# Weights requested in the first turn, and the first image's attention on four pairs of PSUM banks

## The reference

```
Q = Wq x + bq;  K = Wk x + bk;  V = Wv x + bv
attn = softmax(Q^T K / sqrt(128))          # 1024 x 1024 for each image
x = attn V + x
```

## Time and profile before

| | |
|---|---|
| device time, median of 3 runs | 8342.78 us (8341.23 to 8348.9) |
| span of the profiled execution | 8342.4 us |
| TensorE busy | 7778.2 us, 93% |
| GpSimd busy | 7494.7 us, 90% |
| VectorE busy | 7384.7 us, 89% |
| ScalarE busy | 7209.6 us, 86% |
| start of TensorE's first instruction | 22.78 us |
| start of the second turn (image 0) | 134.8 us |

### The profile page before, as it was taken

One profiled execution on the slowest core, in us unless ns is written; L12 is line 12 of the kernel. 1 busy time (PEld: TensorE's weight loads), 2 busy tenths in 40 slices (PEclk: granted clock), 3 DMA queues, 4 the chain that ended last, 5 costly groups with the idle time before them and its releaser, 6 DMA issues. The chain is left out here.

```text
span 8342.4 us, 152469 instructions
## 1 busy us (share of the span) xinstructions
PE 7778.2 (93%) x53376; PEld 6086.4 (73%) x53376; DVE 7384.7 (89%) x10476; ACT 7209.6 (86%) x12224; POOL 7494.7 (90%) x7020
## 2 busy tenths in 40 slices
PE   6999999999999999999999999999999999999986
PEld 4777777777777777777777777777777777777765
DVE  4899999999899999999988999999899999889885
ACT  5898898898888898888888888988889888889874
POOL 3999999999999999999899999999899999899985
PEclk9999999999999999999999999999999999999998
DMA  1222222222222222222222222222222222222221
GB/s 51 75 65 81 76 75 75 72 72 77 75 74 75 72 72 78 75 74 75 68 76 75 75 75 72 73 77 75 73 75 72 73 76 76 73 71 71 77 71 35
DMA packets 322661, 604.29 MB, mean 72 GB/s; under 512 B 42017, under 2 KB 45026, under 8 KB 321890
## 3 DMA queue, kind: packets, MB, share of 16 engines
q1 hardware_dynamic: 321890, 594.45, 23.0%
HBM read 556.55 MB, written 20.97 MB: 69 GB/s over the span
## 5 line engine op out<-in xcount | busy, mean ns | idle before, releaser
L1096 POOL TENSOR_TENSOR g<-h,c_all 128x1024 f32<-128x1024 f32 x2048 | 4858.1, 2372 | 455.0 <-PE ps L530 250.7
L864 ACT ACTIVATE da<-dt,a_neg 128x512 f32<-128x512 f32 x4096 | 2792.6, 714 | 201.2 <-DVE h L1197 195.6
L1197 DVE TENSOR_TENSOR_SCAN h<-da,ps 128x512 f32<-128x512 f32 x2048 | 2423.9, 1208 | 377.6 <-PE ps L526 219.1
L1197 DVE TENSOR_TENSOR_SCAN h<-da,h,ps 128x512 f32<-128x512 f32 x2048 | 2552.0, 1269 | 127.6 <-PE ps L526 48.6
L526 PE MATMUL ps<-ident,ub 128*128 128x128 f32 x16384 | 2397.3, 276 | 240.4 <-DVE h L1197 221.8
L526 PEld LDWEIGHTS ps<-ident,ub 128*128 128x128 f32 x16384 | 1878.9, 142 | 890.3 <-issue 495.6
L530 PE MATMUL ps<-ident,g 128*128 128x128 f32 x16384 | 2253.8, 275 | 14.5 <-POOL g L1096 11.0
L530 PEld LDWEIGHTS ps<-ident,g 128*128 128x128 f32 x16384 | 1897.9, 142 | 462.6 <-issue 431.4
L1082 POOL TENSOR_SCALAR ub<-u_tok,b_tok 128x256 f32<-128x256 f32 x4096 | 1929.3, 486 | 183.1 <-ACT u_tok L953 99.5
L876 ACT ACTIVATE ub<-u_tok,b_tok 128x256 f32<-128x256 f32 x4096 | 1839.6, 498 | 136.9 <-PE ps L526 121.3
L853 ACT ACT_TABLE_LOAD x446 | 572.2, 1283 | 7.9
(11 more groups left out here) (130 smaller groups left out, 9368.8 us busy)
## 6 DMA issues: line engine op xcount, KB each, us to landing
c_all<-c_rows SPq DMA_DIRECT2D x2048, 256.0 KB, 3.1
x_in<-in_x SPq DMA_DIRECT2D x32, 512.0 KB, 5.6
t_old<-t SPq DMA_DIRECT2D x32, 512.0 KB, 4.4
out<-tile_b SPq DMA_DIRECT2D x32, 512.0 KB, 2.9
c_rows<-rows SPq DMA_DIRECT2D x128, 32.0 KB, 2.9
w_conv<-in_conv_rows SPq DMA_DIRECT2D x1, 512.0 KB
f_w<-in_f_w SPq DMA_DIRECT2D x2, 256.0 KB
hid<-in_in_proj SPq DMA_DIRECT2D x1, 256.0 KB
```

The source lines that it names most:

```text
L864: act.activation(da[:, n % 2, half, :], dt[:, slot, half, :], ACT.Exp, scale=a_neg[:, r, half, s:s + 1]).then_inc(da_made, 1)
L1096: pool.tensor_tensor(g[:, n % 2, :, :], h[:, n % 2, :, at:at + BANK], c_all[:, n % RING, :].unsqueeze(1).to_broadcast([P, NH, BANK]), ALU.mult
L1197: dve.tensor_tensor_scan(h[:, n % 2, half, at:at + BANK], da[:, n % 2, half, :], ps[:, DB + half, :], before, ALU.mult, ALU.add).then_inc( ...
```

## The change

Three edits. The list `loads` is built ahead of the first block, and SP issues it in the first turn (before its first wait there) and no longer in the first block. In the first turn `att(i)` goes round four pairs of banks (X, Y and the two that the mixer uses in later turns, DB and YA), and scores wait for the addition of block i-4. The slots of the first turn put the scores of block i+2 between the transposes and the product of block i, and the set-up of the weights further back.

```
-    FIRST_S = tuple(FIRST + 4 * i for i in range(8) for c in range(2))
+    FIRST_PAIRS = 4
+    FIRST_S = tuple(FIRST + 1 + 4 * i for i in range(8) for c in range(2))
...
-    FIRST_PV = tuple(FIRST + 5 + 4 * i for i in range(8) for c in range(2))
+    FIRST_PV = tuple(FIRST + 10 + 4 * i for i in range(8) for c in range(2))
...
-    SETUP = FIRST + 12
+    SETUP = FIRST + 26
...
             def _(sp):
                 with nc.allow_non_contiguous_dma(reason="weights, once"):
                     for dst, src in first_loads:
                         sp.dma_start(dst, src).then_inc(first_loaded, 16)
-                    for dst, src in loads:
-                        sp.dma_start(dst, src).then_inc(loaded, 16)
...
             def att(i):
 
-                return Y if i % 2 and not now else X
+                return X if now else (X, Y, DB, YA)[i % FIRST_PAIRS]
...
+                    if not now and nxt:
+                        with nc.allow_non_contiguous_dma(reason="weights, once"):
+                            for dst, src in loads:
+                                sp.dma_start(dst, src).then_inc(loaded, 16)
                     if joined:
                         sp.wait_ge(v_made, since(v_made, 0))
...
                             if part == 0:
                                 pe.wait_ge(v_kept, since(v_kept, 1))
-                            elif c == 0 and (now or i > 1):
-                                pe.wait_ge(t1_made, since(t1_made, i if now else i - 1))
+                            elif c == 0 and (now or i >= FIRST_PAIRS):
+                                pe.wait_ge(t1_made, since(t1_made, i if now else i - FIRST_PAIRS + 1))
```

More of the change, by code:

```diff
@@ L129, in conv_attn_mamba_mod_kernel @@
     FIRST = SLOTS * 12
-    FIRST_S = tuple(FIRST + 4 * i for i in range(8) for c in range(2))
+    FIRST_PAIRS = 4
+    FIRST_S = tuple(FIRST + 1 + 4 * i for i in range(8) for c in range(2))
     FIRST_MAX = tuple(FIRST + 1 + 4 * i for i in range(8))
-    FIRST_EXP = tuple(FIRST + 1 + 4 * i for i in range(8))
-    FIRST_PT = tuple(FIRST + 4 + 4 * i for i in range(8))
-    FIRST_PTKEEP = tuple(FIRST + 4 + 4 * i for i in range(8))
-    FIRST_PV = tuple(FIRST + 5 + 4 * i for i in range(8) for c in range(2))
-    FIRST_T1 = tuple(FIRST + 6 + 4 * i for i in range(8))
-    SETUP = FIRST + 12
+    FIRST_EXP = tuple(FIRST + 5 + 4 * i for i in range(8))
+    FIRST_PT = tuple(FIRST + 8 + 4 * i for i in range(8))
+    FIRST_PTKEEP = tuple(FIRST + 8 + 4 * i for i in range(8))
+    FIRST_PV = tuple(FIRST + 10 + 4 * i for i in range(8) for c in range(2))
+    FIRST_T1 = tuple(FIRST + 11 + 4 * i for i in range(8))
+    SETUP = FIRST + 26
     def due(slots, g):
@@ L279, in conv_attn_mamba_mod_kernel @@
         weights_made = ctx.enter_context(nc.semaphore("weights_made"))
+        loads = [
+            (in_cols, I["in_proj"][:, :, 0:DI].rearrange("r c e -> c r e")),
+            (w_z[:], I["in_proj"][:, :, DI:2 * DI].rearrange("r c e -> c r e")),
+            (w_conv[:].rearrange("p r k e -> p (r k) e"),
+             I["conv_rows"].rearrange("o (a e) -> o a e", e=DI)[:, :, 0:P].to_broadcast([P, DIRS * KCONV, P])),
+            (w_in[:], I["in_proj"][:, :, P:2 * P].rearrange("r c e -> c r e")),
+            (w_in0[:], I["in_proj"][:, :, 0:P].rearrange("r c e -> c r e")),
+            (w_taps0[:].rearrange("p r k -> p (r k)"),
+             I["conv_rows"].rearrange("o (a e) -> (o e) a", e=DI)[0:P, :]),
+            (w_taps[:].rearrange("p r k -> p (r k)"),
+             I["conv_rows"].rearrange("o (a e) -> (o e) a", e=DI)[P:2 * P, :]),
+            (conv_b[:], I["conv_b"]),
+            (w_dt[0:DR], I["dt_w"][:, :, 0:P]), (w_dt[QUAD:QUAD + DR], I["dt_w"][:, :, P:2 * P]),
+            (b_dt[:], I["dt_b"]),
+            (a_neg[:], I["A_logs"]), (d_skip[:], I["Dp"]), (w_out[:], I["out_w"]),
+            (ln_g[:], I["ln_g"]), (ln_b[:], I["ln_b"]),
+            (w1[:], I["w1"]), (b1[:], I["b1"]), (w2[:], I["w2"]), (b2_rows[:], I["b2"].to_broadcast([P, C])),
+            (wr[:], I["wr"]), (br[:], I["br"].to_broadcast([P, 1])),
+            (f_w1[:], I["f_w1"]), (f_b1[:], I["f_b1"]), (f_w2[:], I["f_w2"]), (f_b2[:], I["f_b2"]),
+            (w_rows[:, :, :, 0:DR + DS], I["x_proj"][:, :, :, 0:DR + DS]),
+            (w_rows[:, :, :, QUAD:QUAD + DR], I["x_proj"][:, :, :, 0:DR]),
+            (w_rows[:, :, :, QUAD + DR:XROWS], I["x_proj"][:, :, :, DR + DS:DR + 2 * DS]),
+        ]
         with nc.Block() as block:
@@ L286, in conv_attn_mamba_mod_kernel @@
                 (wk[:], I["wk"]), (bk[:], I["bk"]), (wv[:], I["wv"]),
[L287 to L309, removed]
             ]
```

## The result

The changed kernel takes 8308.53 us (median of 4 runs, 8304.41 to 8311.75) against 8342.8 before (8341.23 to 8348.9). The ratio is 0.9956, with a 95% interval of 0.9941 to 0.997: 34.3 us less, where 28.3 were forecast. Part of this gap was the draw of the runs. In a second set, with the same kernel beside 28 runs of the kernel before (8326.63 to 8350.15), the ratio was 0.9969 (0.9957 to 0.9981). The mean of all 10 runs of the change is 8309.6 and of the 41 runs of before in all sets 8340.3: **30.8 us less**, with a standard error of 1.9.

What follows compares the result with a forecast made beforehand. Only the first 134.7 us could change, bound by a barrier waiting for SP's weight requests, then attention's three-engine chain. 15.95 + 12.3 = 28.3 us off 8342.4 gave 8314.1, plus 0.4 for timed runs: 8314.5 us, range 8304 to 8324.

Steps and rivals of the forecast that it cites:

- Part (1): Program start: with weights requested behind the barrier, TensorE starts at 6.83 and not 22.78 us, 15.95 us less.
- Part (2): First image's queries, keys and values beside the weight transfers: no cost taken, 0 to 2 us as the doubt.
- That rival: First turn's start: its beginning waits beside the weights, so only attention's 12.3 us stay, 8330 us; chance 4%.
- Part (3): First image's attention: four bank pairs and scores ahead make TensorE the bound, intervals of 4.5 us, 12.3 us less.
- Part (4): Set-up moved on VectorE in the attention: addition of block 4 comes 1.4 us late, nobody waits, no cost.
- Part (5): TensorE's clock in the first turn: zero; bounds 1.9 us less if rising one burst earlier, 5.5 more if later.
- The slow rival: Attention: clock stays at 1.2 GHz, costing 38.0 against 28.3 us won, 8352 us, slower than before; chance 1.5%.

Runs made afterwards that it cites:

- e2: Kernel before with only the attention part changed (four bank pairs, scores ahead, set-up moved), weights still issued in the first block; 8328.91 us, ratio 0.9988.
- e1: Kernel before with only the weight transfers moved behind the barrier; banks, slots and set-up as before; 8318.84 us, ratio 0.9974.
- e3: Changed kernel with 21 GpSimd memsets of unused tiles in the first block, making its barrier late; 8337.04 us, ratio 0.9994.
- e5: Changed kernel with four bank pairs but the slots of before, so scores stand behind the product with v; 8308.95 us, one run.
- e6: Changed kernel with three pairs of banks instead of four; 8299.94 us, one run.
- e7: Changed kernel with 25 unread products filling TensorE's pauses behind the first turn's attention; 8308.36 us, ratio to before 0.9958.
- e8: Changed kernel with e7's filling products plus four products of zeros while the image is loaded; 8298.82 us, ratio to before 0.995.

## Why the prediction was right

**The place.** All of the gain that can be laid to the change lies ahead of the second turn, and the work behind it is the same in count, with TensorE busy for 7705 us after 7711. That held.

**Part (1), 15.95 forecast, 16.12 measured.** Two small errors met. wv landed at 6.20, later than 5.98 and not earlier as I had thought possible; and from VectorE's end to TensorE's start there were 0.31 us, not 0.70. The gap depends on who comes last: 0.70 (before) and 0.69 (e2) where it is SP with its requests, 0.31 (after, e1) and 0.33 (e3) where it is VectorE or GpSimd. The prediction carried the one over to the other. That the 0.22 us and the 0.39 us nearly cancelled was luck. The transfers needed 18.2 us to issue, 18.07 before, and nobody waited for them.

**Part (2), nothing forecast, nothing measured.** The products with wq keep their 3.78 us beside a DMA share of 0.91 in their first half, and the first scores their 3.70 beside 1.00; the products with wk had less beside them (0.32 in 14 to 20 us). The gap at the branch into the turn, 0.31 us, was shorter than before. (The prediction took the queue as quiet at this branch in the kernel before; the DMA share there was 0.77.) The Trainium skill (Runtime: NRT & Kernel Launch, Instruction fetch mechanics) says that a taken branch to a page that isn't held has to fetch it by DMA first. No such fetch shows here: in 0 to 34.5 us of this trace the two queues for instructions moved nothing, and the profile lists only the data queue. That rival fell.

**Part (3), 12.3 forecast, 13.0 measured.** The mechanism was right in each link: TensorE became the bound, the copy and the exponential came in time, the last interval stayed at 4.04. The mis-sized term is the product with v in the sum of one interval: I took its 1.89 us from a row in which it starts from standstill, and in the row without waits it is 1.79. With transposes 0.88 and scores 1.71 that makes 4.38, where the prediction had 4.48 and rounded it up to 4.5, six times. e5 shows that TensorE's order carries 8.3 of the 13.0, e6 that three pairs carry nearly all of it.

**Part (4), nothing forecast, nothing measured**, and for the reason given. e6 shows the other side: with three pairs TensorE does wait for that addition, and it costs 1.1 us.

**Part (5), zero with bounds.** In the profiled pair it was zero: the clock rose at the same burst. But in the profiles of e1, e5 and e6 it rose one burst earlier (1.8 us) and in e7 within the products with wv (1.4 late), with nothing changed ahead of it there. So the bounds were real, and a sum of this turn is not good to better than 2 us.

**The slow rival** was summed a little too low: five intervals at the low level make 5.5 + 5 x 4.48 = 27.9 us, which is not yet the 28.3 won. No run came near it.

**The sum.** 28.3 forecast; 29.1 in the first turn of the profiles; 30.8 with an error of 1.9 in the means of all runs; 34.3 in the first four. The last lies inside the range, but for a reason that the range didn't have: I had the stretch behind the first turn fixed within 5 us, and it lies between 8192 and 8215 in the ten profiled executions. The gain of the first turn is what the prediction got right by its mechanism; where in the range four runs fall beyond that is the draw. I also set the profiled execution 0.4 us below its timed figure; in the later sets the two differ by 1.8.

## What to carry to other kernels

An order on one engine and the buffers that allow it are two edits, and both the gain and the need can be read from one chain: place the next item's independent work where the bound engine waits for another, and count how far ahead the buffer must be free. A barrier costs what its last comer does; requests for data that nobody needs yet belong behind it. And where a short stretch of a long kernel is changed, compare that stretch in the traces: here the ends of the first turn agreed within 0.1 us between the two profiled executions of the change, while the whole time of the kernel before spread over 24.6. But read the clock's rise in that stretch too: where it came at another burst, the end moved by 1.4 to 1.8 us with nothing changed.

## What the runs showed of the hardware

The level of TensorE's clock at the start of a program is not fixed by the program: with the same bursts it rose ahead of the second (14.8 us in e1) or ahead of the third group of products (19.9 us with the change), and in e7 in the middle of the third. Of the nine executions without products ahead of the image, three (e1, e5, e6) have it ahead of the second group, five ahead of the third. Four products of zeros from 1.31 to 5.94 us were enough to have it at the upper level at 6.67 in the one profiled execution of e8, and products in the pauses kept it there through most of what follows the attention (mean level 0.96 in 57 to 98 us, where the changed kernel has 0.60 in 62 to 103). This work that nobody reads took 9.3 us off the first turn. The granted clock in the windows reads 1.00 from the program's start in all traces, so that the low level there shows only in the bursts' durations, 3.78 against 1.98.

The DMA engines' work beside TensorE cost it nothing that the rows show: 3.70 us for eight score products beside a share of 1.00, and 3.70 in the kernel before. And a meeting of all engines at the end of the first block took 0.31 to 0.33 us from the last comer where that was VectorE or GpSimd, and 0.69 to 0.70 where it was SP.
